# Cross-attention and 4-bit feed-forward on one core: FFN rows placed by DMA, and x2 ahead of q's third pair on GpSimd

## The reference

```
xn  = layernorm(x)                                   # over the 1024
q   = softmax over 64 channels of each head (Wq xn) * 64**-0.5
k   = softmax over 1024 tokens (Wk ctx);  v = Wv ctx
att = Wo (context(k, v) q) + bo
x   = x + att / norm(att) * g * sqrt(128)
x   = x + layernorm(x) @ w + bias                    # w = (4-bit integers - zero point) * scale
```

## Time and profile before

| | us |
|---|---|
| median of 3 runs | 703.54 |
| lowest and highest | 703.54, 704.14 |
| profiled execution, its own time | 706.99 |
| its span, first to last instruction | 704.9 |
| mean granted TensorE clock, as a share of full | 0.978 |

### The profile page before, as it was taken

How to read it: one execution, slowest core, us unless ns; L and a number is a source line. 1 busy time by engine, 2 the same in 40 slices (tenths; PEclk the granted TensorE clock), 3 DMA queues, 4 the chain that set the end, 5 groups by cost and what they waited for, 6 DMA issues and landing times.

```text
span 704.9 us, 11155 instructions
## 1 busy us (share of the span) xinstructions
PE 654.4 (93%) x3312; PEld 420.1 (60%) x3328; DVE 555.5 (79%) x900; ACT 449.6 (64%) x747; POOL 474.5 (67%) x406
## 2 busy tenths in 40 slices
PE   4858799999999999999999999999999999999987
PEld 3635556666666666656666666666666665666543
DVE  2997778888878788888878888888878887887844
ACT  3575666767585767667485666758575766748432
POOL 2166286776949496785949677694949678594820
PEclk9989889999999999999999999999999999999989
DMA  8125236363553637263454636255363724344451
GB/s 297 62 52 120 54 54 171 91 152 59 149 113 83 164 89 179 50 173 74 119 126 96 166 89 163 50 154 105 80 161 89 179 53 116 69 114 78 92 106 60
DMA packets 178871, 78.43 MB, mean 111 GB/s; under 512 B 168328, under 2 KB 169888, under 8 KB 178848
## 3 DMA queue, kind: packets, MB, share of 16 engines
q1 hardware_dynamic: 172512, 55.09, 36.9%
q10 hardware_dynamic: 6336, 23.07, 9.7%
HBM read 28.32 MB, written 8.39 MB: 52 GB/s over the span
## 4 chain that ended last, share of the span: by engine, by line
PE 34%; POOL 25%; issue 19%; DVE 12%; ACT 7%; DMA 1%; POOLq 0%; another core or an unknown queue 0%; DVEq 0%; ACTq 0%; SPq 0%
PE ps_m L1268 6%; POOL q_tok_lo L429 6%; POOL x L510 3%; POOL q_exp L419 3%; PE ps_m L1180 3%; POOL c_lo L473 3%; DVE q_sum L859 3%; POOL y L435 3%; PE ps_k L1110 3%; PE ps_o L1110 2%; POOL rn L492 2%; PE ps_k L1112 2%; PE ps_o L1111 2%; PE ps_k L1111 2%; PE ps_o L1112 2%
## 5 line engine op out<-in xcount | busy, mean ns | idle before, releaser
L429 POOL TENSOR_TENSOR q_tok_lo<-q_exp,q_tok_hi 128x1024 f16<-128x1024 f32 x64 | 140.0, 2189 | 85.8 <-ACT q_tok_hi L574 85.8
L419 POOL TENSOR_TENSOR q_exp<-q_exp,q_rec 128x1024 f32<-128x1024 f32 x64 | 122.2, 1910 | 5.0
L1180 PE MATMUL ps_m<-k_t,c_t 128*128 128x512 f32 x256 | 119.8, 602 | 0.0
L563 ACT ACTIVATE q_exp<-q_exp 128x512 f32<-128x512 f32 x128 | 80.5, 629 | 45.9 <-DVE q_exp L852 45.9
L840 DVE TENSOR_REDUCE k_nmax<-ps_k 128x1 f32<-128x1024 f32 x64 | 78.1, 1220 | 40.1 <-PE ps_k L1112 40.0
L558 ACT ACTIVATE k_exp<-ps_k,k_nmax 128x1024 f32<-128x1024 f32 x64 | 71.1, 1110 | 55.1 <-DVE k_nmax L840 55.1
L574 ACT ACTIVATE q_tok_hi<-q_exp 128x1024 f16<-128x1024 f32 x64 | 67.6, 1056 | 49.8 <-POOL q_exp L419 49.8
L847 DVE TENSOR_REDUCE q_nmax<-ps_q 128x8 f32<-128x512 f32 x128 | 87.3, 682 | 11.2 <-PE ps_q L1112 9.6
L852 DVE TENSOR_TENSOR q_exp<-ps_q,q_nmax 128x512 f32<-128x512 f32 x128 | 88.5, 692 | 5.1 <-DVE q_nmax L847 0.2
L1110 PE MATMUL ps_q<-wq_hi,xn_lo 128*128 128x512 f32 x128 | 74.4, 581 | 9.7 <-DVE q_exp L852 7.0
L417 POOL TENSOR_TENSOR q_rec<-q_rec,q_range 128x16 f32<-128x16 f32 x64 | 15.6, 244 | 93.3 <-DVE q_rec L862 93.3
(11 more groups left out here) (185 smaller groups left out, 1385.1 us busy)
## 6 DMA issues: line engine op xcount, KB each, us to landing
x_res<-in_x ACTq DMA_DIRECT2D x16, 512.0 KB, 3.4
out_x<-y SPq DMA_DIRECT2D x15, 512.0 KB, 2.9
x_in<-in_x ACTq DMA_DIRECT2D x14, 512.0 KB, 4.7
c_in<-in_ctx ACTq DMA_DIRECT2D x14, 512.0 KB, 6.0
x_in<-in_x SPq DMA_DIRECT2D x2, 512.0 KB, 6.0
c_in<-in_ctx SPq DMA_DIRECT2D x2, 512.0 KB, 8.1
q_hi<-q_tok_hi SPq DMA_TRANSPOSE x64, 3.1
q_lo<-q_tok_lo SPq DMA_TRANSPOSE x64, 3.1
```

Of the source, the lines that this page charges most:

```text
L419: nc.gpsimd.tensor_tensor(pair, pair, rec.unsqueeze(2).to_broadcast([P, 2 * HEADS, DH]), ALU.mult).then_inc(qs_done, 1)
L429: nc.gpsimd.tensor_tensor(q_tok_lo[p % 2][:], q_exp[:, 2 * p:2 * p + 2, :].rearrange("p t d -> p (t d)"), q_tok_hi[p % 2][:], ALU.subtract ...
L563: nc.scalar.activation(q_exp[:, j, :], q_exp[:, j, :], ACT.Exp).then_inc(qexp_done, 1)
L1180: last = nc.tensor.matmul(ps_m[:], c_t[s][:, t, :], k_t[:, t, :], start=(t == 0), stop=(t == TC - 1))
```

## The change

1. **Rows by DMA.** scale_bc is loaded by one broadcasting DMA. The zero and bias rows stay 8 x 128, are split there in three bf16 parts (ACT, POOL; six small operations in all with DVE's), and SP places them with 12 small DMAs in ffn_rows, which POOL clears at the start. PE's 27 transposes, ACT's seven copies and the mixing and splitting in iteration 1 go.
2. **Nibbles.** The second buffer is a tile of its own, nibble, not x_res. Four nibbles are picked and converted in iteration 0 (DVE steps 1, 3, 5, 6; ACT steps 2, 4, 6, 7) and four in iteration 1 (DVE steps 1, 2, 3, 5; ACT steps 2, 3, 4, 6). ACT copies vo out, not DVE.
3. **Iteration -1.** DVE's list becomes: statistics of x, maximum of the context, xn, the weights' low parts, the rows, the first k maximum. fit_x comes ahead of c_lo on POOL, the high part of xn ahead of wo_t on ACT, project_k(0, 0) ahead of the second transposes of the context on PE.
4. **Order in every iteration.** On POOL: xn_lo, x2's additions, scale_q(a, 2), fit_x2(c), low_q(a, 2). On ACT: high_q(c, 2) behind move_m in the next iteration, exp_k(a, 1) ahead of high_q(c, 3), the loads behind the squares in step 4. On DVE: sum_q(a, 3) behind x2's statistics. On SP: q's pair 2 high, x2 high, pair 2 low, pair 3 high, x2 low, pair 3 low. The last full iteration (END) keeps the old order.
5. gs_undo is a tensor_scalar with gs_col as its scalar, not a tensor_tensor of two columns.

```diff
@@ sync
             load_c(1, 1)
+            sp.dma_start(scale_bc[:], scales.rearrange("o a -> (a o)").partition_broadcast(P)).then_inc(scale_spread, 16)
+            sp.wait_ge(consts_made, 10)
+            for part in range(3):
+                sp.wait_ge(rows_split, (1, 3, 4)[part])
+                for r in range(4):
+                    row = 32 * part + r
+                    sp.dma_start(ffn_rows[row:row + 1, :].rearrange("a (t c) -> a t c", t=TC),
+                                 row_parts[:, r // 3, part, :]).then_inc(rows_placed, 16)
...
+                if do_c:
+                    turn_q(c, 2, "hi")
                 if do_f:
                     sp.wait_ge(x2hi_done, f + 1)
...
                 if do_c:
+                    turn_q(c, 2, "lo")
                     turn_q(c, 3, "hi")
...
-                if do_a:
+                if isinstance(i, int) and i == END:
                     turn_q(a, 2, "hi")
                     turn_q(a, 2, "lo")
@@ gpsimd
+                if isinstance(i, int) and i == 0:
+                    both = rows_in[:, 1:3, :]
+                    pool.wait_ge(rows_split, 1)
+                    nc.gpsimd.tensor_tensor(both, both, row_parts[:, :, 0, :], ALU.subtract).then_inc(rows_split, 1)
+                    pool.wait_ge(rows_split, 3)
+                    nc.gpsimd.tensor_tensor(row_parts[:, :, 2, :], both, row_parts[:, :, 1, :],
+                                            ALU.subtract).then_inc(rows_split, 1)
                 for j in range(STEPS):
-                    if j == 0 and do_f:
-                        fit_x2(f)
...
-                    if j == 6 and do_a:
+                    if j == 6 and isinstance(i, int) and i == END:
                         scale_q(a, 2)
...
+                    if j == 7 and do_a and not (isinstance(i, int) and i == END):
+                        scale_q(a, 2)
+                    if j == 7 and do_c and not (isinstance(i, int) and i == END):
+                        fit_x2(c)
                     if j == 7 and do_a:
                         low_q(a, 2)
@@ scalar
+                    if j == 0 and isinstance(i, int) and i == 0:
+                        act.wait_ge(zero_steps, 5)
+                        nc.scalar.activation(row_parts[:, :, 0, :], rows_in[:, 1:3, :], ACT.Copy).then_inc(rows_split, 1)
                     if j == 0 and do_c:
                         move_m()
-                    if j == 0 and do_c:
-                        if begun(c):
-                            act.wait_ge(x2_done, 2 * c)
-                            nc.scalar.dma_start(x_res[:], x[c]).then_inc(xres_loaded, 16)
...
+                        high_q(c, 2)
                     if j == 0 and do_f:
                         normalise_x2()
...
                     if j == 0 and do_f:
                         high_x2()
+                    if j == 0 and do_a:
+                        exp_k(a, s, 1)
                     if j == 0 and do_c:
                         high_q(c, 3)
...
+                    if j == 4 and do_c:
+                        if begun(c):
+                            act.wait_ge(x2_done, 2 * c)
+                            nc.scalar.dma_start(x_res[:], x[c]).then_inc(xres_loaded, 16)
+                    if j == 4 and (not isinstance(i, int) or 0 <= i < NB - 2):
+                        act.wait_ge(xn_done, i + 1)
+                        nc.scalar.dma_start(x_in[s][:], x[i + 2]).then_inc(x_loaded[s], 16)
...
+                        nc.scalar.dma_start(c_in[s][:], ctx_in[i + 2]).then_inc(c_loaded[s], 16)
...
-                    if j == 6 and do_a and not (isinstance(i, int) and i == END):
-                        high_q(a, 2)
-                    if isinstance(i, int) and i == 0:
-                        set_up_ffn(j)
...
+                    if isinstance(i, int) and i == 0 and j == 0:
+                        move_vo()
                         act.wait_ge(rows_split, 2)
-                        nc.scalar.activation(ffn_rows[32:64, :], bias_bc[32:64, :], ACT.Copy)
-                        nc.scalar.activation(ffn_rows[64:96, :], bias_bc[64:96, :], ACT.Copy).then_inc(rows_split, 1)
+                        nc.scalar.activation(row_parts[:, :, 1, :], rows_in[:, 1:3, :], ACT.Copy).then_inc(rows_split, 1)
+                    if isinstance(i, int) and i == 0 and j in (2, 4, 6, 7):
+                        convert_nibble((2, 4, 6, 7).index(j))
                     if isinstance(i, int) and i == 1 and j == 0:
-                        convert_nibble(2 * RC - 1)
-                        act.wait_ge(w_converted, 2 * RC)
                         nc.scalar.dma_start(x_res[:], x[c]).then_inc(xres_loaded, 16)
+                    if isinstance(i, int) and i == 1 and j in (2, 3, 4, 6):
+                        convert_nibble(4 + (2, 3, 4, 6).index(j))
@@ vector
-                    nc.vector.tensor_tensor(gs_undo[:], g_undo[:], gs_col[:], ALU.mult).then_inc(fit_steps, 1)
+                    nc.vector.tensor_scalar(gs_undo[:], g_undo[:], gs_col[:], None, ALU.mult).then_inc(fit_steps, 1)
...
+                if isinstance(i, int) and i == FIRST:
+                    stats_x()
+                    mean_x()
+                    abs_c()
+                    norm_x()
+                    set_up()
                     set_up_rows()
+                    top_c()
+                    max_k(n, 0)
+                    return
...
+                    if j == 7 and do_a and not (isinstance(i, int) and i == END):
+                        sum_q(a, 3)
@@ tensor
                     if isinstance(i, int) and i == 0:
                         if j == 0:
                             pe.wait_ge(ctop_done, 1)
                             set_up_vo()
-                            set_up_cols()
-                        elif j < 4:
-                            set_up_row(2 * (j - 1))
-                            set_up_row(2 * (j - 1) + 1)
...
+                    if j == 7 and do_n and isinstance(i, int) and i == FIRST:
+                        project_k(n, 0)
                     if j == 7 and do_n:
                         transpose_c(1)
```

More of the change, by code:

```diff
@@ L89, in build @@
         scale_bc = sb("scale_bc", [P, OUT])
-        zero_bc = sb("zero_bc", [P, OUT])
-        bias_bc = sb("bias_bc", [P, OUT])
+        nibble = sb("nibble", [P, OUT])
         bo_col = sb("bo_col", [P, 1])
@@ L162, in build @@
         q_packed = [t[:].bitcast(I32) for t in (og, sq, spare, x2)]
[L163 removed]
+        q_nibble = [t[:].bitcast(I32) for t in (y, nibble)]
         rows_in = sb("rows_in", [TC, 3, P])
         inv_scale = sb("inv_scale", [TC, P])
[L166 removed]
+        row_parts = sb("row_parts", [TC, 2, 3, P], BF16)
         k_flat = k_t[:].rearrange("p t h -> p (t h)")
@@ L286, in loads @@
             return 8 * (b - s) + 16
+        NIBBLES = [(m + 2 * late, high) for late in range(2) for high in range(2) for m in range(2)]
         FIRST, LAST = -1, NB + 2
@@ L470, in iteration @@
                         low_q(a, 0)
-                    if j == 3 and do_n:
-                        pool.wait_ge(chi_done, n + 1)
-                        nc.gpsimd.tensor_tensor(c_lo[:], c_in[1 - s][:], c_hi[:].bitcast(F32),
-                                                ALU.subtract).then_inc(clo_done, 1)
+                    if j == 3 and do_n and not first:
+                        low_c()
                     if j == 4 and do_a:
@@ L523, in set_up, with move_vo @@
                 nc.scalar.activation(wq_hi[:], ps_q[:], ACT.Copy).then_inc(whi_done, 1)
+            def move_vo():
+                act.wait_ge(vo_ready, 1)
+                for q in range(2):
+                    nc.scalar.activation(vo[:].rearrange("p (k q o) -> p q k o", q=2, o=P)[:, q],
+                                         ps_o[q][:].rearrange("p (k o) -> p k o", k=HC), ACT.Copy).then_inc(vo_moved, 1)
             def set_up_rest():
@@ L534, in convert_nibble @@
                 act.wait_ge(nibble_done, k + 1)
-                nc.scalar.activation(w_int[:, k // RC, k % RC], q_nibble[k % 2], ACT.Copy).then_inc(w_converted, 1)
-            def set_up_ffn(j):
-                if j == 0:
-                    act.wait_ge(cols_ready, 1)
-                    nc.scalar.activation(cols[:].rearrange("p k t -> p (k t)"), ps_m[:, 0:3 * TC],
-                                         ACT.Copy).then_inc(cols_moved, 1)
-                if 1 <= j < 4:
-                    row = (scale_bc, zero_bc, bias_bc)[j - 1]
-                    for h in range(HALVES):
-                        act.wait_ge(rows_ready, 2 * (j - 1) + h + 1)
-                        nc.scalar.activation(halves(row)[h], ps_o[h][:], ACT.Copy).then_inc(rows_moved, 1)
-                if j > 0:
-                    convert_nibble(j - 1)
+                m, high = NIBBLES[k]
+                nc.scalar.activation(w_int[:, high, m], q_nibble[k % 2], ACT.Copy).then_inc(w_converted, 1)
             def iteration(i, s, do_n, do_a, do_c, do_f):
@@ L559, in exp_k, with high_x @@
```

(8 more changed lines are left out.)

208 lines of the change are left out of this document (89 added, 119 removed).

## The result

Over four runs each on one chip, the changed kernel takes 685.37 us (684.52 to 685.74), the kernel before 703.59 (703.54 to 704.14): a ratio of 0.9738, 95% interval 0.9721 to 0.9754, 18.2 us less. A later comparison of the same two on one chip gave 685.41 against 704.41, 0.9729 (0.9709 to 0.9749). The forecast was 686.0 in a range of 676 to 697. The profiled execution of the changed kernel took 685.74 us, its span is 683.9; that of before took 706.99, its span is 704.9. So the two traces differ by 21.0 us, and only some 18 to 19 of it are there in typical runs.

The account below looks back on a forecast made before the run. PE bounds the loop, chains over DVE, ACT and GpSimd iterations 0 and 1. Terms -6.0 - 7.5 - 5.1 = -18.6 took the median 703.54 to 684.9; with 1 us given back for the clock, 686.0 us, range 676 to 697.

Parts of the forecast that it names:

- 1 for the clock: 1 us given back because some work in the new iterations 0 and 1 will run at the lower clock.
- Part A: Opening: with xn first, project_q(0) starts about 18.2 us; the rows' load costs nothing, about 3.5 us if landing at 18.7.
- Part B: Iteration 0: three things leave the chain to the next project_q(0), which ends near 54.2, not 60.2: -6.0 us.
- 2.1 us for scale_q(2): Iteration 0: scale_q(2), with q_rec ahead of it, no longer stands ahead of xn_lo, saving 2.1 us.
- Part C: Iteration 1: two-tile mixing and splitting go, four nibbles come; it lasts 39.5 us, not 47.0: -7.5 us.
- the bound of 42.5: Iteration 1's upper bound in us: each of four nibbles held up, half of it hidden.
- Part D: Loop: exp_k starts 1.4 us earlier and all PE waits for it go, -5.1 us; g_lo's waits stay.
- rival 4: Every iteration: scale_q(2), last on POOL, comes late and ACT holds the work behind high_q(2); slower, 708 us, chance 0.06.
- 2, the port: Loop: low_x2 on DVE runs beside POOL's scale_q(3), losing 0.4 us an iteration, 5.6 in all; 691.6 us, chance 0.07.
- 1: Loop gains nothing, as PE waits instead at g_lo or the next exp_k; 691 us, chance 0.10.
- 5: More gain: g_lo's waits go too and the head runs cleaner; 678 us, chance 0.08.
- 3: Head: another chain takes over and halves the gain; 691.5 us, or 696 with the loop's gain lost; chance 0.11.

Follow-up runs that it names:

- Experiment 4: Changed kernel with the old order in every iteration, keeping the rows, nibbles, vo copy, iteration -1 list and gs_undo changes: 693.91 us, ratio 0.9835.
- experiment 9: Changed kernel with scale_q(2) ahead of xn_lo on GpSimd in iteration 0 only: 684.88 us beside 685.41 for the changed kernel.
- experiment 8: Changed kernel with other places for the nibble picks and conversions in iterations 0 and 1: 681.97 us, ratio 0.9666; run again, 682.68 beside 685.41.
- experiment 5: Changed kernel with the old order in every iteration, but exp_k(a, 1) ahead of high_q(c, 3): 688.81 us, ratio 0.9767.
- experiment 1: Kernel before with one move alone, exp_k(a, 1) ahead of high_q(c, 3) on ACT: 698.5 us, ratio 0.9898.
- experiment 2: Changed kernel with exp_k(a, 1) behind high_q(c, 3) again: 700.06 us, ratio 0.9911.
- experiment 6: Changed kernel with the x_res, x_in and c_in loads issued in step 0 again, behind high_q(c, 2): 740.75 us, ratio 1.0507.
- experiment 3: Changed kernel with the old order from iteration 2 on and the loads in step 0 there: 699.45 us, ratio 0.9898.

## Why the prediction was right, and where it was not

**The sum** held: 686.0 forecast, 685.4 measured. That it came so close is luck: a gain taken too small in the loop and gains taken too large in the head offset each other. Experiment 4 against before, and the changed kernel against experiment 4, give the split in typical runs by ratios: all but the new order 0.0165 of 705.5, or 11.6 us (forecast for the head 13.5 less 1 for the clock, 12.5); the new order 0.9835 - 0.9729, or 7.5 us (forecast for the loop 5.1).

**Part A, opening.** Right: 18.15 against 18.2. The rows' load had landed: the reciprocal ran at 12.41 us with no idle time before it. The opening's timeline of DVE and GpSimd, which answers the earlier trace rows:

```profile
12.41 0.93 DVE L809 RECIPROCAL inv_scale<-rows_in 8x128 f32<-8x128 f32 x1
13.38 1.37 DVE L811 TENSOR_TENSOR rows_in<-rows_in,inv_scale 8x128 f32<-8x128 f32 x1
14.78 2.28 DVE L813 TENSOR_SCALAR rows_in<-rows_in 8x128 f32<-8x128 f32 x1
...
14.56 2.42 POOL L522 TENSOR_TENSOR xn_lo<-xn,xn_hi 128x1024 fp32r<-128x1024 f32 x1
```

I had counted these operations as small. One of 128 columns took 2.28 us and ended only when xn_lo did, another 1.37 beside c_lo. The k maximum came at 17.78 where it was 17.60 before, so there was just room for it. The Trainium skill (SBUF — State Buffer, Who interferes with whom) names two kinds of DVE operations that a GpSimd instruction issued before them blocks for its whole length: those with two SBUF inputs, as in the row of 1.37 us, and two-port ones, tensor_scalar among them, as in the row of 2.28. Both rows agree, and an operation on 8 partitions is no exception.

**Part B, iteration 0.** End forecast at 54.2, measured at 54.41, but the agreement is luck in part: the step "2.1 us for scale_q(2)" failed (experiment 9). The conversion of a nibble in the changed iteration 0 (ACT), and the iteration's end (GpSimd, then PE):

```profile
34.19 1.05 ACT L572 ACTIVATE w_int<-y 128x1024 f16<-128x1024 int32 x1
...
50.48 2.39 POOL L522 TENSOR_TENSOR xn_lo<-xn,xn_hi 128x1024 fp32r<-128x1024 f32 x1 [2.02 <-ACT xn_hi L591]
...
52.24 2.74 PE L1200 MATMUL ps_m<-k_t,c_t 128*128 128x512 f32 x6
54.41 0.80 PE L1130 MATMUL ps_q<-wq_hi,xn_lo 128*128 128x512 f32 x1
```

Xn_lo was ready at 52.87; PE was busy until 54.4. I had followed one chain to its end and not asked when PE itself would be through. PE was late from a place that I had not costed: the conversion of a nibble (34.19, 1.05 us) stands ahead of the k_t copies on ACT, PE waited 3.79 us for them until 35.86 (2.84 with the conversion elsewhere, experiment 8), and then worked partly at the lower level of its clock (0.58 from 42 to 46 us). The iteration 0 of experiment 4, then that of experiment 5, which has the same instructions there:

```profile
16.33:54.26 37.93, 29.85 (x125) 19.80 (x124) 29.31 (x46) 24.94 (x40) 20.03 (x15) 0.82 0.31 83
17.06:53.30 36.24, 28.39 (x124) 19.20 (x123) 30.30 (x46) 24.39 (x40) 18.62 (x15) 0.91 0.32 81
```

So the clock that an execution happens to get is worth 1.7 us of this iteration, and at 0.91 it is as long as the changed kernel's 36.26, though scale_q(2) stands ahead in it. That the other steps of Part B (the zero_bc copies, the nibbles ahead of xn) gave what they were priced at is argued, not shown.

**Part C, iteration 1.** 39.5 forecast, 41.06 measured, inside the bound of 42.5. The 38.7 us from which the forecast starts is not worked out from a row. The nibbles were held up, as the bound supposed: 1.84 and 2.51 us for two of the four.

```profile
L840 DVE TENSOR_SCALAR nibble<-x 128x1024 int32<-128x1024 int32 x2 | 4.3, 2173 | 0.0
L840 DVE TENSOR_SCALAR nibble<-sq 128x1024 int32<-128x1024 int32 x2 | 1.4, 686 | 0.0
```

But their places cost 0.6 us at the same clock, and the lower clock 1.7, by experiment 8: with other places and a clock of 0.96 the iteration lasts 38.98. For the clock I had given back 1 us in both iterations together, so the term that was mis-sized most is the clock.

**Part D, the loop.** The mechanism is shown by experiments 1, 2 and 5: exp_k's place gives most of it, the rest of the order 0.31 us a pair. G_lo's waits stayed, as forecast. The size was wrong: 5.1 us are the idle times in the earlier trace rows, but the loop gave 8.0. Aligned instruction by instruction, PE's starts before and after fall apart in one place of an iteration only, project_k(2) behind mix_out(0): by 0.25 us in one and 0.85 in the next, 1.1 per pair, seven pairs 7.7. There, in the kernel before, the idle time printed was 0.61, and the matmul ahead of project_k started here:

```profile
275.52 0.38 PE L1112 MATMUL ps_o<-q_hi,g_hi 128*128 128x512 f16 x1
```

The starts lay 276.51 - 275.52 = 0.99 us apart, where the matmuls of this group follow each other at 0.22. The end of a matmul is modelled, and an idle time counted from it leaves out a part of the stall. The "slack" of 1.1 us from high_x2 to the k maximum is seen as ACT's 0.98 wait.

**The loads** were the real gap: I priced their move by ACT's idle time, as free. It is not a nicety but what the new order stands on; left in step 0 they cost 55 us (experiment 6). My rival 4, a slowdown by scale_q(2), had the right sign of danger at the wrong resource. I had read the loads' landing times and the transposes' as separate rows and never laid them over each other.

**The rivals.** 2, the port, is there by its size: x2n_lo takes 1.64 us on average where it took 1.23, 0.4 an iteration, as put. But it is not on the path: none of PE's starts behind it shifts against before. 1 and 5 fall by g_lo's unchanged 3.8 us and the exp_k waits gone; 3 by experiment 4.

## What to carry to other kernels

When an order gets several moves at once, price them together and one by one: here exp_k's place was worth twice as much in the new order as in the old, the new order was a loss without it, and one overlooked companion move (the loads) decided the sign of the whole. Where a bound engine waits, read the distance from start to start of its instructions, not the idle time alone. And end each chain with the question what the bound engine itself is doing at that time: a chain that leaves 1.5 us to spare gives nothing when it is shortened.

## What the runs showed of the hardware

- Of DMA transposes issued close together on SP beside three loads of 512 KB, the later ones are stretched: the issue took 6.24 us in the rows of experiment 6 and 4.73 in experiment 3 where it takes 1.23 to 1.33, the landing of the one ahead went from 2.7 to 8.5 us in the median, the last load's from 6.0 to 11.1. In the rows shown of the kernel before, one transpose beside the same loads took 1.29.
- Iteration 1 of one and the same kernel took 38.98 us in one execution, at a granted clock of 0.96, and 40.68 in another, at 0.92; iteration 0 of the same instructions took 36.24 us at 0.91 and 37.93 at 0.82.
- DVE's product of two columns takes 1.00 us on average with both read from SBUF, 0.21 with one as scalar operand, in the same place beside GpSimd.
